# Eight residual layers in one program: the last layer's products, softmax and stores by chunks of three batches, and the row length of two attentions by column tiles

## What is computed

```python
Q, K, V = (x @ Wq, x @ Wk, x @ Wv)
energy = jnp.einsum('bqd,bkd->bqk', Q, K)
lengths = jnp.sum(energy[:, 0] != 0, axis=-1)
pad = kidx[None, None, :] >= lengths[:, None, None]
```

```python
gate = jax.nn.softmax(xt @ gate_w.T, axis=-1)
base = xt @ weight.T
t = jnp.einsum('nh,erh->ner', xt, lora_U)
lora = jnp.einsum('ne,eor,ner->no', gate, lora_V, t)
out = base + lora / 16
```

## Time and profile before

| what | us |
|---|---|
| the three runs | 1205.83, 1214.05, 1220.04 |
| the profiled execution's own time | 1209.49 |
| its span, from first to last instruction | 1207.6 |
| two attentions, in the span | about 742 to 841 |
| last layer, first transpose to last add | 1172.59 to 1202.59 |
| store of `x`, issued | 1203.38 |

### The profile page before, as it was taken

The page is one execution under the profiler, slowest core; times in us unless marked ns, Lnnn a source line. Parts: engine busy times, 40 slices in busy tenths (PEclk is TensorE's granted clock), DMA queues, the critical chain, the costliest instruction groups (busy, mean ns, idle before and its releaser), DMA issues. The chain is left out here.

```text
span 1207.6 us, 26748 instructions
## 1 busy us (share of the span) xinstructions
PE 970.9 (80%) x10817; PEld 642.7 (53%) x10845; DVE 744.0 (62%) x2025; ACT 576.3 (48%) x945; POOL 391.7 (32%) x418
## 2 busy tenths in 40 slices
PE   4999799998999977988897763785657577489987
PEld 2677333433333424776675562563456466447766
DVE  3586666546655464653574134468899999557752
ACT  3465465644555425644652631665535354235531
POOL 4320200000000022775002665146576656333340
PEclk9899799998999988998896886987878788789987
DMA  6000000000000016000000322000000000000000
GB/s 268 2 2 2 19 1 1 0 1 0 1 0 1 0 41 240 2 4 2 2 3 12 96 68 92 1 1 1 2 2 3 1 3 3 2 1 2 2 2 36
DMA packets 14713, 27.77 MB, mean 23 GB/s; under 512 B 1024, under 2 KB 12416, under 8 KB 13696
## 3 DMA queue, kind: packets, MB, share of 16 engines
q1 hardware_dynamic: 13568, 23.97, 5.5%
q0 software_dynamic: 1024, 2.10, 0.6%
HBM read 20.17 MB, written 5.90 MB: 22 GB/s over the span
## 5 line engine op out<-in xcount | busy, mean ns | idle before, releaser
L1324 PE MATMUL l0f_ctl<-l1f_in,l0f_in 128*128 128x512 f32 x320 | 145.7, 598 | 0.5
L548 DVE TENSOR_REDUCE l_neg_max<-l_ring 128x4 f32<-128x512 f32 x128 | 82.1, 684 | 63.5 <-PE l_ring L410 62.9
L128 POOL TENSOR_SCALAR row_var_eps<-row_mean_var 128x12 f32<-128x12 f32 (+2 forms) x16 | 3.7, 230 | 362.5 <-DVE row_mean_var L123 361.8
L2600 ACT COPY l2f_blocks_sb<-l2f_right_t_sb 32x1024 f32<-32x1024 f32 x64 | 66.8, 1043 | 86.6 <-PE l2f_given_ps L2531 75.5
L507 ACT ACTIVATE l_probs<-l_scores 128x1024 f32<-128x1024 f32 x64 | 65.6, 1025 | 82.2 <-PE l_scores L418 82.2
L1324 PEld LDWEIGHTS l0f_ctl<-l1f_in,l0f_in 128*128 128x128 f32 x320 | 61.7, 193 | 71.4 <-issue 70.2
L2531 PE MATMUL l2f_given_ps<-l2f_blocks_sb,l2f_left_t_sb 128*32 128x128 f32 x1024 | 50.1, 376 | 40.1 <-DVE l2f_hid_sb L2700 35.6
L2531 PEld LDWEIGHTS l2f_given_ps<-l2f_blocks_sb,l2f_left_t_sb 128*32 128x32 f32 x1024 | 44.0, 153 | 54.0 <-issue 53.8
L698 POOL TENSOR_TENSOR l_squares<-l_exps 128x1024 f32<-128x1024 f32 x32 | 60.6, 1895 | 29.8 <-ACT l_exps L953 29.8
L1045 DVE TENSOR_REDUCE l_neg_max<-l_scores 128x8 f32<-128x1024 f32 x32 | 39.2, 1225 | 43.4 <-PE l_scores L750 43.4
L368 POOL TENSOR_SCALAR_AFFINE_SELECT l_probs<-l_probs 128x1024 f32<-128x1024 f32 x32 | 35.0, 1094 | 64.0 <-ACT l_probs L507 64.0
(11 more groups left out here) (466 smaller groups left out, 2635.2 us busy)
## 6 DMA issues: line engine op xcount, KB each, us to landing
l1f_in<-in_l1f SPq DMA_DIRECT2D x1, 4580.0 KB, 13.5
l0f_in<-in_l0f SPq DMA_DIRECT2D x1, 2302.5 KB, 8.4
l1f_in<-in_l2u SPq DMA_DIRECT2D x1, 2048.0 KB, 8.7
sorted_rows<-first_in SPq DMA_DIRECT2D x1, 1856.0 KB, 10.4
l0f_in<-in_l2f SPq DMA_DIRECT2D x1, 1792.5 KB, 18.0
l1f_sorted<-sorted_rows SPq DMA_DIRECT2D x7, 256.0 KB, 4.9
expert_rows<-l1f_sorted SPq DMA_DIRECT2D x7, 256.0 KB, 2.2
x_in<-in_x SPq DMA_DIRECT2D x1, 1024.0 KB, 4.9
```

The lines of the kernel that those rows point to most:

```text
L548: ring.free(V.tensor_reduce(out, score_bank(b, half, g), AX.X, ALU.max, negate=True), ("score", b, half, g))
L1324: return nc.tensor.matmul(out, lhs, rhs, start=start, stop=stop)
L2600: A.copy(blocks[rows, :, u, :], right_t[rows, :, :]).then_inc(blocks_made, 1)
```

## The change

In the last layer, gate and down matrix are stored side by side, and one product of 136 columns per batch gives both. Batches now go in chunks of three, since three times 136 columns fit in a bank. That is six chunks: five of three batches, and one with a single batch, whose two empty slots are filled by products that repeat batch 15, so that the logits of all slots can be read. The softmax runs in two halves of nine slots. The base products of the first two chunks are issued before the first transpose of low-rank values. From then on, in each round PE transposes the next chunk, makes the base products of the next chunk, and then the up products of this one. The bank of base and up products alternates between two, and the base product of chunk k+1 waits for the add of chunk k-1. SP stores each chunk of `x` as soon as it is added: five DMAs of 192 KB and one of 64 KB, inside the layer. The last block is gone.

In the two attentions the stage `length` is gone. The count is made by four products of 32 stationary columns (queries 0 to 31) with all 128 keys moving, each into its own 32 partitions of the bank. They are issued before the scores. DVE makes 0 or 1 of the whole 128x128 bank, sums along the row, and writes a 128x512 bf16 tile whose rows 0, 32, 64 and 96 hold the mask of batches 0 to 3. The mask is one product of 512 columns with a 0/1 matrix that picks those rows. A table of 128x512 (`key_of_row`) and the 0/1 matrix are loaded with the weights of the sixth layer, 288 KB more in a DMA whose end is waited for during the fourth layer. 128 KB less are loaded at the start.

```diff
@@ gated_lora
+            def project(slot):
+                ins = mm(both[:, slot // PER, slot % PER, :], xnT[:, min(slot, B - 1), :], w["down_gate"][:, :],
+                         start=True, stop=True)
+                if slot + 1 in (HALF * PER, CHUNKS * PER):
+                    ins.then_inc(both_made, 1)
+            def base(k):
+                if k < 2:
+                    norm.wait_stored(pe, NCH - 2 + k)
+                else:
+                    pe.wait_ge(added, k - 1)
+                for q, b in enumerate(batches(k)):
+                    mm(turn_ps[k % 2][:, q, :], xnT[:, b, :], w["weight"][:, :], start=(q == 0), stop=False)
-            for i in range(NCH):
-                for q in range(4):
-                    ins = mm(low_ps[i][:, q, :], xnT[:, 4 * i + q, :], w["down"][:, :], start=True, stop=True)
-                ins.then_inc(projected, 1)
-            for i in range(NCH):
-                pe.wait_ge(low_made, i + 1)
...
-                pe.wait_ge(flip_stored, i + 1)
-                for q in range(4):
-                    o = out_ps[i % 2][:, q, :]
-                    mm(o, xnT[:, 4 * i + q, :], w["weight"][:, :], start=True, stop=False)
-                    ins = mm(o, low_t[i][:, q, :], w["up"][:, :], start=False, stop=True)
-                ins.then_inc(out_made, 1)
+            base(0)
+            base(1)
+            flip(0)
+            for k in range(CHUNKS):
+                if k + 1 < CHUNKS:
+                    flip(k + 1)
+                    if k:
+                        base(k + 1)
+                widen(k)
...
+            shift_down(0)
+            share(0)
+            lower(0)
+            shift_down(1)
+            for k in range(1, HALF):
+                lower(k)
+            share(1)
+            for k in range(HALF, CHUNKS):
+                lower(k)
+                add(k - HALF)
+            for k in range(CHUNKS - HALF, CHUNKS):
+                add(k)
...
+            for k in range(CHUNKS):
+                sp.wait_ge(added, k + 1)
+                sp.dma_start(held(m["out"], k), held(x, k)).then_inc(stored, 16)
+            sp.wait_ge(stored, 16 * CHUNKS)
@@ two_attentions
-    ATTEND = ("project", "values", "scores", "length", "mask", "top", "exp", "flip", "pv", "stats", "scale", "turn")
+    ATTEND = ("project", "values", "scores", "mask", "top", "exp", "flip", "pv", "stats", "scale", "turn")
+                    for q in range(4):
+                        ins = mm(counts.bank((a, c))[32 * q:32 * q + 32, 0, :], qT[c][:, q, 0:32], keys[a][c][:, q, :],
+                                 start=True, stop=True)
+                    counts.fill(ins, (a, c))
...
+                    scores.fill(mm(scores.bank((a, c))[:, :, :], fold_of["first_rows_bf"][:, :], neg[c][:, :, :],
+                                   start=False, stop=True), (a, c))
...
+                counts.free(V.tensor_scalar(nonzero[c][:, :], counts.bank((a, c))[:, 0, :], 0.0, None, ALU.not_equal), (a, c))
+                counts.wait_freed(dve, (a, c), 0)
+                own(V.tensor_reduce(length[c][:, :], nonzero[c][:, :], AX.X, ALU.add))
+                V.tensor_scalar(neg[c][:, :, :], fold_of["key_of_row"][:, :, :], length[c][:, 0:1], NEG, ALU.is_ge, ALU.mult) \
```

More of the change, by code:

```diff
@@ new lines, in gated_lora @@
+        neg_top, total, inv = sb("neg_top", slots), sb("total", slots), sb("inv", slots)
+        below, exps, gate = sb("below", slots + [E]), sb("exps", slots + [E]), sb("gates", slots + [E])
+        low, low_t = sb("low_rank", slots + [P]), sb("low_t", slots + [S])
+        both_ps = ps("both", [P, CHUNKS, 4 * S])
+        turn_ps = [ps(f"turn{k}", [P, 4, S]) for k in range(2)]
+        both = both_ps[:, :, 0:PER * BOTH].rearrange("p c (q n) -> p c q n", n=BOTH)
+        both_made, below_made, exps_made, step = \
+            [new_semaphore(f"{tag}_{n}") for n in ("both_made", "below_made", "exps_made", "step")]
@@ new lines, in base, with flip @@
+            def base(k):
[5 more added lines that the diff above has]
+                    mm(turn_ps[k % 2][:, q, :], xnT[:, b, :], w["weight"][:, :], start=(q == 0), stop=False)
+            def flip(k):
+                pe.wait_ge(low_made, k + 1)
+                for q, b in enumerate(batches(k)):
+                    ins = nc.tensor.transpose(both_ps[:, k, q * S:q * S + S], low[:, b, :], identity[:, :])
+                ins.then_inc(flipped, 1)
@@ new lines, in widen @@
+            def widen(k):
+                pe.wait_ge(flip_stored, k + 1)
+                for q, b in enumerate(batches(k)):
+                    ins = mm(turn_ps[k % 2][:, q, :], low_t[:, b, :], w["up"][:, :], start=False,
+                             stop=(b == batches(k)[-1]))
+                ins.then_inc(out_made, 1)
+            norm.pe(pe, 0)
+            norm.pe(pe, 1)
+            for i in range(NCH):
+                norm.wait_stored(pe, i)
+                for b in range(4 * i, 4 * i + 4):
+                    project(b)
+                if i + 2 < NCH:
+                    norm.pe(pe, i + 2)
@@ L2087, in _, with part, logits, by_chunk @@
-            for i in range(NCH):
-                add(i)
+            def part(h):
+                return slice(h * HALF * PER, (h + 1) * HALF * PER)
+            def logits(h):
+                return both[:, h * HALF:(h + 1) * HALF, :, P:BOTH]
+            def by_chunk(a):
+                return a.rearrange("p (c q) e -> p c q e", q=PER)
+            def each_gate(row, h):
+                return row[:, part(h)].unsqueeze(2).broadcast_to([P, HALF * PER, E])
+            def shift_down(h):
+                dve.wait_ge(both_made, h + 1)
+                chain(V.tensor_reduce(neg_top[:, part(h)].rearrange("p (c q) -> p c q", q=PER), logits(h), AX.X, ALU.max,
+                                      negate=True))
+                V.tensor_tensor(by_chunk(below[:, part(h), :]), logits(h), by_chunk(each_gate(neg_top, h)), ALU.add) \
+                    .then_inc(below_made, 1)
@@ new lines, in share, with lower @@
+            def share(h):
+                dve.wait_ge(exps_made, h + 1)
+                chain(V.tensor_reduce(total[:, part(h)], exps[:, part(h), :], AX.X, ALU.add))
+                chain(V.reciprocal(inv[:, part(h)], total[:, part(h)]))
+                chain(V.scalar_tensor_tensor(gate[:, part(h), :], exps[:, part(h), :], 1.0 / R, each_gate(inv, h),
+                                             ALU.mult, ALU.mult))
+            def lower(k):
+                n = len(batches(k))
+                V.tensor_tensor(held(low, k).rearrange("p q (e r) -> p q e r", r=R),
+                                both[:, k, 0:n, 0:P].rearrange("p q (e r) -> p q e r", r=R),
+                                held(gate, k).unsqueeze(3).broadcast_to([P, n, E, R]), ALU.mult).then_inc(low_made, 1)
```

125 lines of the change are left out of this document (38 added, 87 removed).

## The result

The changed kernel took 1195.21 us (median of 1195.23, 1193.84, 1196.66 and 1195.19), the kernel before 1210.26 with a fourth run beside the three shown. The ratio is 0.9876, 95% interval 0.9841 to 0.9910. Run again later on another occasion it was 0.9880 (0.9846 to 0.9913). The forecast was 1200, the range 1191 to 1209. So the direction was right and the time lies inside the range, but outside the forecast case (1200 within 3 us). The size was a sixth too small: the spans of the two profiled executions differ by 14.1 us (1207.6 and 1193.5), and the sum said 11.8.

The account below looks back on a forecast made before the run. PE was taken to bound the last layer, PE then ACT the first attention, with DVE waits in the second. Gains of 8.1, 1.8 and 1.9 made 11.8 us; from 1211.8 this gave 1200 us, range 1191 to 1209.

Parts of the forecast that it names:

- the sum: Whole kernel: gains of 8.1 us in the last layer, 1.8 and 1.9 in the two attentions, 11.8 us together.
- Products of the last layer: Last layer's 136-column passes: 0.20 us each at low clock, clock rising at 1180.5, all 18 slots done at 1182.3.
- First add: Last layer: DVE's add of chunk 0, late behind the second half's softmax steps and fourth low_rank, ends at 1187.1.
- The circle: Last layer: up products, handover, add, way back and base products form a closed round of 2.3 us per chunk.
- Stores: End of last layer: storing by chunks leaves 3.5 us after the last add against 5.0, 1.5 less (0.5 to 2.0).
- First attention: Cheaper counts, no length products and mask changes on PE bring everything until the second attention's scores 1.8 us earlier.
- the slower rival: Clock falls in the first attention before 785 and stays low through the second; 1216.5 us in all, chance 0.05.
- Second attention: Its first transpose starts at 798.1 instead of 800.01: 1.9 us more gain, with 0.5 and 2.6 as ends.
- The rival with the clock up: Second attention: clock stays full, three transpose steps save 0.87 each, 2.6 us more, giving 1197; chance 0.2.
- all moves along: Second attention from 802 on: ACT, DVE and POOL set the pace, and the earlier gain carries through.
- The low clock until 1188: Rival for the last layer: clock rises no earlier than before, layer gives about 6 us, 1202 in all; chance 0.15.
- That counts do not overlap: Rival in both attentions: count passes follow each other, total gain 8.6 us instead of 11.8, giving 1203; chance 0.05.

Follow-up runs that it names:

- Cutting the circle: Changed kernel with sums of the last layer's chunks 2 to 5 in free PSUM banks, so base products skip the add's wait: 1192.55 us, ratio 0.9846 to before.
- narrow ones: Changed kernel with an 8-column gate product ahead of every 136-column product in the last layer: last layer 36.4 us instead of 24.1.
- early down products: Kernel before with each chunk's down products right behind its gate products in the last layer: ratio 1.0042, last layer 39.9 us instead of 35.0.
- gates last: Kernel before with the last layer's down products between the transposes and all gate products behind them: last layer 37.6 us instead of 35.0.

## Why the prediction was right, and where not

1. **Products of the last layer: right direction, size off, and the reason for the clock was too weak.** The pass at half clock was taken at 0.20 and cost 0.227, inside the bounds. The 0.188 of a down pass, from which the estimate came in part, is a mean over both clocks: in the trace of before the starts are 0.213 us apart until the clock rises at 1187.9, and 0.111 behind that. The rise was moved by the 8.3 us between first wide products, to 7.9 us behind the first transpose. It came at 4.8. The experiments show that narrow products hold the clock down. Whether the transposes ahead of the wide products bring the rise forward is not shown: behind the first wide product it came 2.8 us here and 4.8 before. All 18 slots were done at 8.7 us instead of 9.7, which is 1.0 us.
2. **First add: the step that failed.** "What is late next is thus the first add", behind the second half's softmax and fourth `low_rank`. The prediction has DVE ready for it 13.9 us behind the layer's first transpose and PE at 13.0. Measured were 11.4 and 11.9: DVE had begun earlier and with shorter steps (0.23 us for nine slots, before 0.29 for sixteen), and waited 0.50 us for PE. The first add ended at 12.45, not 14.5. With point 1 that is 2.1 us.
3. **The circle: right.** The prediction has 2.3 us, and 2.25 were measured. Cutting the circle gave rounds of 1.67 us and a layer 2.6 us shorter.
4. **Stores: right, 0.6 too little.** The tail is 2.9 us, predicted 3.5, before 5.0. The gain of 2.1 lies just over the stated upper end of 2.0. The tail was given 0.3 for the issue and 2.0 for the transfer behind it; the page counts from the issue, and the last store landed 1.8 us behind that. The stores by chunks alone are worth 1.85.
5. **First attention: 1.8 predicted, 1.46 measured, 0.6 kept.** The count passes cost 0.1 more each, the 512-column mask holds PE as long as the four small ones did. The fall of the clock took back 0.86. It is the trigger of the slower rival (before 785), but the clock was full again by 774.8 instead of staying low, so 0.9 us and not 11.5.
6. **Second attention.** At its first transpose 2.2 us of the predicted 3.7 had been won. The rival with the clock up, given 0.2, came true, with steps of 2.68, 2.74 and 2.74. But "three steps save 0.87 each" misreads, where the step from 800.01 to 802.75 is already 2.74. Two steps were slow, and the clock was worth 1.8 us and not 2.6. Of the 4.1 us at the fourth transpose POOL's round, which the prediction left at "all moves along", gave back 1.0. That 3.2 stands against the predicted 3.7 is luck: a fall of the clock, a rise of it and POOL's round, none of them in the sum, nearly cancelled.
7. **Rivals.** The low clock until 1188 was seen in none of the eight profiled executions with the changed products (narrow ones not added). That counts do not overlap is refuted.

The sum was 2.3 us short: 2.8 in the last layer and 0.2 ahead of the attentions, less 0.5 in them and 0.2 in the seventh layer. The forecast of 1200 began from 1211.8, and the median of before with all four runs was 1210.3. So of the 4.8 us between forecast and result 1.5 are the starting point, 2.3 the sum, and 1.0 the scatter of the runs.

## What to carry to other kernels

A few narrow products can cost more than their passes: look at what they do to the granted clock of the wide ones around them, and fold them into a wide product if they can be. Where base, add and next base share two banks, look for banks that an earlier stage has already left. And a gain ahead of a closed round of another engine (here POOL's) is worth only what that round does not take back.

## What the runs showed of the hardware

- PE can be busy for 17 us without a pause at 1.2 GHz, if 8-column products stand between 128-column ones (early down products, 1173.5 to 1191, half of the passes on `xnT` wide). With transposes and 136-column products alone full clock came 4.8 us behind the layer's first transpose in the changed kernel.
- Eight-column f32 passes cost what 128-column ones do: their starts are 0.213 us apart at half clock (both in before) and 0.111 to 0.112 at full clock (both in gates last). Passes of 136 columns are 0.227 and 0.116 apart.
- Products on different groups of 32 output columns overlap although they use the same rows: 0.034 us each round the groups, 0.077 where the same product is repeated.
- A DVE step of 128x4 took 0.17 us, and 1.17 beside POOL's 128x512 step.
- The same program gets different clocks at the same place from one execution to the next: 113.7 or 124.0 us for a layer that is the same in both, 3.19 or 2.74 between two transposes behind the same idle time.
